# Router logits from widened embedding and hidden-turn matmuls, and the gating moved to earlier slots

## What is computed

```python
h = x_patch @ W.T + b                                   # embedding, D = 64
hid_t = tanh(layernorm(h) @ W_ih.T + b_ih + b_hh + hid_{t-1} @ W_hh.T)
h = h + hid_t                                           # called h2 in the kernel
x2 = layernorm(h)                                       # no scale, no shift
logits = x2 @ gate_w + gate_b                           # 16 experts
top2, idx = top_k(logits, 2); w = softmax(top2)
moe = sum_k w_k * (relu(x2 @ w1[idx_k] + b1[idx_k]) @ w2[idx_k] + b2[idx_k])
out = h + layernorm(x2 + moe) * gamma + beta
```

## Time and profile before

| | |
|---|---|
| three runs | 575.0 us median (574.65 to 578.51) |
| profiled execution | 573.36 us, of which its span is 571.6 us |
| mean granted TensorE clock | 0.987 |
| busy share of the span | PE 92%, DVE 75%, ACT 62%, POOL 27% |
| the chain that ended last | 86% PE, 5% DVE, 4% ACT |

### The profile page before, as it was taken

One profiled execution on the slowest core, in us unless ns is written; L12 is line 12 of the kernel. 1 busy time (PEld: TensorE's weight loads), 2 busy tenths in 40 slices (PEclk: granted clock), 3 DMA queues, 4 the chain that ended last, 5 costly groups with the idle time before them and its releaser, 6 DMA issues.

```text
span 571.6 us, 8948 instructions
## 1 busy us (share of the span) xinstructions
PE 526.4 (92%) x3138; PEld 358.3 (63%) x3138; DVE 428.4 (75%) x819; ACT 351.9 (62%) x596; POOL 155.2 (27%) x133
## 2 busy tenths in 40 slices
PE   2565999999999999999999999999999999989982
PEld 2355667667676767667676767666676766656541
DVE  1135787888888988788888888887878888786771
ACT  1244565666857585666757585666767585756552
POOL 4105021321314141331314141332214141221334
PEclk9999999999999999999999999999999999999995
DMA  3403865481909365482909375472909274563701
GB/s 79 100 1 79 194 139 120 103 183 49 234 24 198 85 148 133 100 179 57 227 22 203 80 155 118 116 171 62 224 20 210 75 160 104 122 145 91 168 1 42
DMA packets 30140, 67.45 MB, mean 118 GB/s; under 512 B 7056, under 2 KB 12432, under 8 KB 29968
## 3 DMA queue, kind: packets, MB, share of 16 engines
q1 hardware_dynamic: 30096, 66.89, 51.0%
HBM read 59.59 MB, written 7.28 MB: 117 GB/s over the span
## 4 chain that ended last, share of the span: by engine, by line
PE 86%; DVE 5%; ACT 4%; issue 2%; SPq 1%; POOL 1%; DMA 1%; POOLq 0%; DVEq 0%; ACTq 0%
PE pZ L711 32%; PE pO L724 31%; PE pA L735 4%; PE pA L660 4%; PE pB L635 4%; ACT hexp L426 2%; PE pA L653 2%; PE pB L686 2%; PE pA L675 2%; PE pA L645 1%; DVE acc L559 1%; PE pB L695 1%; SPq L293 1%; PE pB L675 1%; PE pA L654 1%
## 5 line engine op out<-in xcount | busy, mean ns | idle before, releaser
L426 ACT ACTIVATE hexp<-pZ,b1c 128x784 f32<-128x784 f32 x256 | 223.9, 909 | 105.2 <-PE pZ L711 105.0
L543 DVE SCALAR_TENSOR_TENSOR prod<-pO,b2c,spread 128x392 f32<-128x392 f32 x256 | 151.6, 623 | 85.2 <-PE pO L724 79.8
L724 PE MATMUL pO<-hexp,w2s 128*64 128x392 f32 x1024 | 198.5, 504 | 0.3 <-DVE prod L543 0.3
L711 PE MATMUL pZ<-xt,w1hi 128*128 128x392 f32 x512 | 191.3, 374 | 3.8 <-ACT hexp L426 2.7
L711 PE MATMUL pZ<-xt,w1lo 128*128 128x392 f32 x512 | 174.5, 341 | 0.0
L711 PEld LDWEIGHTS pZ<-xt,w1hi 128*128 128x128 f32 x512 | 96.7, 189 | 60.8 <-issue 28.1
L327 POOL TENSOR_TENSOR inv_std<-var,nhalf 112x7 f32<-112x7 f32 x48 | 75.1, 1572 | 216.0 <-DVE var L477 216.0
L559 DVE TENSOR_TENSOR acc<-acc,prod 128x784 f32<-128x784 f32 x112 | 121.0, 1080 | 0.1
L724 PEld LDWEIGHTS pO<-hexp,w2s 128*64 128x64 f32 x1024 | 70.0, 136 | 73.9 <-issue 62.2
L711 PEld LDWEIGHTS pZ<-xt,w1lo 128*128 128x128 f32 x512 | 97.1, 190 | 0.0
L334 POOL TENSOR_TENSOR h2b<-h2c,bet 112x448 f32<-112x448 f32 x16 | 17.4, 1087 | 145.2 <-DMA h2c<-h_dram 145.2
(11 more groups left out here) (74 smaller groups left out, 433.1 us busy)
## 6 DMA issues: line engine op xcount, KB each, us to landing
spread<-gates_dram SPq DMA_DIRECT2D x128, 392.0 KB, 8.6
h_dram<-h SPq DMA_DIRECT2D x16, 199.1 KB, 2.5
h2c<-h_dram SPq DMA_DIRECT2D x16, 199.1 KB, 8.2
xcur<-x_in SPq DMA_DIRECT2D x16, 196.0 KB, 8.1
out<-yo SPq DMA_DIRECT2D x16, 196.0 KB, 7.9
w1f<-w SPq DMA_DIRECT2D x2, 512.0 KB, 6.0
w2s<-w SPq DMA_DIRECT2D x1, 512.0 KB, 6.8
gates_dram<-gt SPq DMA_DIRECT2D x16, 28.0 KB, 2.0
```

Source lines behind the costliest of these rows:

```text
L426: nc.scalar.activation(hexp[u % RING][:, :].rearrange("p (b c) -> p b c", b=2), halves(pZ[u % 2]), ACT.Relu, bias=b1c[:, u:u + 1])\
L543: nc.vector.scalar_tensor_tensor(out=prod[q % RING][:, b * HALF:(b + 1) * HALF], in0=halves(pO)[:, b, :], scalar=b2c[:, q:q + 1], in1=spre ...
L711: last = nc.tensor.matmul(halves(pZ[e % 2])[:, b, :], w[:, e, :], xt[par][:, b * HALF:(b + 1) * HALF], start=(k == 0), stop=(k == 1))
L724: last = nc.tensor.matmul(halves(pO)[k * D:(k + 1) * D, b, :], w2s[:, e, :], hexp[e % RING][:, b * HALF:(b + 1) * HALF], start=True, stop= ...
```

## The change

The gate weights, centred, are appended to the matrices that embedding and hidden turn use, so that both write 16 more columns: the logits of h2 before it is divided by its standard deviation. The widened tiles (81 columns) don't fit one bank, so four tiles go to pA and three to pB, for both. DVE multiplies the 16 columns of h2 with the reciprocal deviation and adds the bias. The `logits` matmuls and the split of the gate weights go. `embed_in` moves from slot 7 to 9, `sum_turn` from 9 to 11, its copy on ACT from 10 to 12, `bias_logits` and `find_first` from 3 to 1, `find_second` from 5 to 3, the exponential from 6 to 4, `gate_weights` from 7 to 5, and `gates_turn` with the copy `gt` from 10 to 6. In bodies -2 and -1 the slots differ (`after(t, fill, steady)`).

```diff

+    W = D + 1 + E
-        tokw = sb("tokw", [K_IN + 1, D + 1])
+        tokw = sb("tokw", [K_IN + 1, W])
...
+        def wide_tile(i):
+            return wide_tiles(pA, PAIRS)[:, i, :] if i < PAIRS else wide_tiles(pB, TILES - PAIRS)[:, i - PAIRS, :]
+        wide_halves = ((slice(0, PAIRS), wide_tiles(pA, PAIRS)),
+                       (slice(PAIRS, TILES), wide_tiles(pB, TILES - PAIRS)))
...
                 if gate:
                     spread_gates(t + 1, 1 - par)
+                if mix and not known(t, 0):
+                    keep_h2(t + 2)
...
-                nc.scalar.activation(h1[par][:, :, :], tiles_and_mean(pB), ACT.Copy).then_inc(EMBED.sem, 1)
+                for some, fresh in wide_halves:
+                    nc.scalar.activation(h1[par][:, some, :], fresh, ACT.Copy).then_inc(EMBED.sem, 1)
+                    if gate and u == after(t, 3, 4):
+                        GATE.wait(act, t + 1, "diff")
+                        nc.scalar.activation(tv[:, 5, :], tv[:, 4, :], ACT.Exp).then_inc(GATE.sem, 1)
+                    if gate and u == after(t, 4, 6):
+                        GATE.wait(act, t + 1, "turned")
+                        ...
+                        nc.scalar.activation(gt[:, :], pB[0:2 * E, 0:FIRST], ACT.Copy).then_inc(GATE.sem, 1)
-                    if embed and u == after(t, 4, 7):
+                    if embed and u == after(t, 6, 9):
                         keep_h1(t + 3, 1 - par)
-                    if close and u == 10:
+                    if close and u == 12:
                         close_center(t - 1)
                         square(CLOSE, t - 1, "center", 2, cen[:, :, :])
...
             def bias_logits(s):
-                GATE.wait(dve, s, "logits")
-                nc.vector.tensor_tensor(lg[:, :, :], parts[:, 0, :, :], over_tiles(gbias[:, :], E), ALU.add)
+                MIX.wait(dve, s, "rstd")
+                nc.vector.tensor_tensor(lg[:, :, :], h2[:, :, D + 1:W], over_e(inv_std[:, 1, :]), ALU.mult)
-                nc.vector.tensor_tensor(lg[:, :, :], parts[:, 1, :, :], lg[:, :, :], ALU.add)
+                nc.vector.tensor_tensor(lg[:, :, :], lg[:, :, :], over_tiles(gbias[:, :], E), ALU.add)
-                    if gate and u == 3:
+                    if gate and u == 1:
                         bias_logits(g)
                         find_first(g)
+                    if gate and u == 3:
+                        find_second(g)
                     if gate and u == 5:
-                        find_second(g)
-                    if gate and u == 7:
                         gate_weights(g)
                     if mix and u == 7:
-                        nc.vector.tensor_tensor(h2[:, :, :], tiles_and_mean(pA), h1[par][:, :, :], ALU.add)
+                        for some, fresh in wide_halves:
+                            nc.vector.tensor_tensor(h2[:, some, :], fresh, h1[par][:, some, :], ALU.add)
...
             def embed_in(s):
-                    GATE.wait(pe, s - 2, "biased")
+                    MIX.wait(pe, s - 1, "h2")
             def hidden_turn(s):
                 MIX.wait(pe, s, "hid")
+                    GATE.wait(pe, s - 1, "gt")
-            def logits(s, par):
-                for i in range(TILES):
-                    last = nc.tensor.matmul(pB[0:P, i * 2 * E:(i + 1) * 2 * E], xt[par][:, i * P:(i + 1) * P],
-                                            gwhl[:, :], start=True, stop=True)
-                    if gate and u == 3:
-                        logits(t + 1, 1 - par)
-                    if gate and u == 10:
-                        gates_turn(t + 1, embed, close)
+                    if gate and u == after(t, 4, 6):
+                        gates_turn(t + 1)
-                    if embed and u == after(t, 4, 7):
+                    if embed and u == after(t, 6, 9):
                         embed_in(t + 3)
-                    if close and u == 9:
-                        sum_turn(t - 1, 1 - par, mix)
+                    if close and u == 11:
+                        sum_turn(t - 1, 1 - par, embed, mix)
```

More of the change, by code:

```diff
@@ L97, in vit_tower_kernel @@
         xcur = sb("xcur", [K_IN + 1, TOK])
-        h1 = [sb(f"h1_{i}", [P, TILES, D + 1]) for i in range(2)]
+        h1 = [sb(f"h1_{i}", [P, TILES, W]) for i in range(2)]
         xn1 = sb("xn1", [P, TILES, D])
         state = sb("state", [2 * D, 2, FIRST])
-        h2 = sb("h2", [P, TILES, D + 1])
+        h2 = sb("h2", [P, TILES, W])
         x2 = sb("x2", [P, TILES, D])
@@ L138, in wait @@
                 eng.wait_ge(self.sem, step * len(self.stages) + self.stages.index(stage) + 1)
-        EMBED = Chain("embed_stage", "h1 kept square var rstd norm turned xn1t_odd xn1t")
-        MIX = Chain("mix_stage", "pre hid_odd hid hid_turned h2 square var rstd x2 hi lo "
+        EMBED = Chain("embed_stage", "h1 kept_front kept square var rstd norm turned xn1t_odd xn1t")
+        MIX = Chain("mix_stage", "pre hid_odd hid hid_turned h2_front h2 square var rstd x2 hi lo "
                                  "turned_a turned_b xt_a xt_b")
-        GATE = Chain("gate_stage", "logits hi_part biased max1 hit1 ranked1 first1 best1 without "
+        GATE = Chain("gate_stage", "scaled biased max1 hit1 ranked1 first1 best1 without "
                                    "max2 hit2 ranked2 first2 best2 diff exp den p1 p2 g1 g2 gates turned gt")
@@ L214, in vit_tower_kernel @@
             cell_loads += [(cell[rows, k, :], w_ih), (cell[rows, 1 - k, :], w_hh),
-                           (rbias[rows, 0:1], b_ih.unsqueeze(1)), (rbias[rows, 1:2], b_hh.unsqueeze(1)),
-                           (gwf[rows, :], gate_w)]
+                           (rbias[rows, 0:1], b_ih.unsqueeze(1)), (rbias[rows, 1:2], b_hh.unsqueeze(1))]
             expert_loads += [(w1f[rows, :, :], w1)]
@@ L279, in body @@
                     fetch_h2(t - 1)
[L280 to L283, removed]
+                if known(t, 0):
+                    if mix:
+                        keep_h2(t + 2)
+                    if gate:
+                        load_x(t + 4)
                 if gate:
                     spread_gates(t + 1, 1 - par)
+                if mix and not known(t, 0):
+                    keep_h2(t + 2)
                 if close:
@@ L484, in bias_logits @@
             def bias_logits(s):
-                GATE.wait(dve, s, "logits")
-                parts = pB[0:P, 0:TILES * 2 * E].rearrange("p (i k e) -> p k i e", e=E, k=2)
-                nc.vector.tensor_tensor(lg[:, :, :], parts[:, 0, :, :], over_tiles(gbias[:, :], E), ALU.add)\
+                MIX.wait(dve, s, "rstd")
+                nc.vector.tensor_tensor(lg[:, :, :], h2[:, :, D + 1:W], over_e(inv_std[:, 1, :]), ALU.mult)\
                     .then_inc(GATE.sem, 1)
-                GATE.wait(dve, s, "hi_part")
-                nc.vector.tensor_tensor(lg[:, :, :], parts[:, 1, :, :], lg[:, :, :], ALU.add).then_inc(GATE.sem, 1)
+                GATE.wait(dve, s, "scaled")
+                nc.vector.tensor_tensor(lg[:, :, :], lg[:, :, :], over_tiles(gbias[:, :], E), ALU.add)\
+                    .then_inc(GATE.sem, 1)
             def find(s, k):
@@ L581, in body @@
                             dve.wait_ge(h2_stored, 16 * s)
-                        nc.vector.tensor_tensor(h2[:, :, :], tiles_and_mean(pA), h1[par][:, :, :], ALU.add)\
-                            .then_inc(MIX.sem, 1)
+                        for some, fresh in wide_halves:
+                            nc.vector.tensor_tensor(h2[:, some, :], fresh, h1[par][:, some, :], ALU.add)\
+                                .then_inc(MIX.sem, 1)
+                    if gate and u == 3:
+                        find_second(g)
                     if gate and u == 5:
-                        find_second(g)
-                    if gate and u == 7:
                         gate_weights(g)
@@ L621, in _ @@
             pe.wait_ge(consts, FOLD_SET)
-            nc.tensor.matmul(pA[0:K_IN + 1, 0:D + 1], tokt[:, :], fold[0:D, :], start=True, stop=True)\
-                .then_inc(tokw_made, 1)
+            for k in range(2):
+                last = nc.tensor.matmul(pA[k * D:(k + 1) * D, 0:E], fold[0:D, 0:D], gw[:, :], start=True, stop=True)
+            last.then_inc(weights_made, 1)
+            pe.wait_ge(weights_made, 2)
+            nc.tensor.matmul(pB[0:K_IN + 1, 0:W], tokt[:, :], fold[0:D, :], start=True, stop=True)\
+                .then_inc(weights_made, 1)
             pe.wait_ge(consts, ONES_SET)
-            pe.wait_ge(tokw_made, 2)
+            pe.wait_ge(weights_made, 4)
             def embed_in(s):
                 pe.wait_ge(xload, 16 * s + 16)
-                if not known(s, 2):
-                    GATE.wait(pe, s - 2, "biased")
-                elif not known(s, 1):
-                    EMBED.wait(pe, s - 1, "xn1t")
+                if not known(s, 1):
+                    MIX.wait(pe, s - 1, "h2")
                 for i in range(TILES):
```

(24 more changed lines are left out.)

44 lines of the change are left out of this document (17 added, 27 removed).

## The result

The changed kernel takes 660.5 us (four runs, 658.2 to 661.2) against 575.0 us beside it: 1.145 times the time of before, 95% interval 1.141 to 1.150. The forecast was 636 with a range to 658: the direction and the places were right, two prices too small.

A forecast was written before the change was run, and what follows sets the result against it. PE alone was taken to set the pace, 32.04 us per step. To the profiled 573.4 us came 48.9 (twelve full steps of +3.6, plus bodies 0, 13 and 14) and 14 for the clock: 636 us, range 604 to 658.

The forecast's parts named there:

- The gates' turn: Slot 6: PE is due at 10.1 us, DVE's gates are ready at 13.6, so PE stands 3.5 us per full step.
- 1.94 (318.93 to 320.87): Length in us taken for `find_second` in DVE's 12.6 us chain to the gates, from the rows of before.
- nobody waits: SP's queue: gate spread issued ahead of `keep_h2`; h2 is needed two bodies on, so no wait was expected.
- The clock: PE's granted clock falls in two in three of 14 stands, 1.5 us lost each, 1.0 per step: +14 us.
- Rival (b): PE's clock falls in every stall and takes long to come back: 656 us, chance 0.13.
- The closing norm: Slot 12: DVE stands 2 us for the closing square, PE about 1.1 before first layer 1; net +0.85 us per step.
- The logits and the wide columns: PE: removed logits matmuls gain 0.77 us in each of bodies 0 to 14; sixteen more columns cost 0.
- Fill and drain: Fill 0, between -3 and +3 us; body 0 +1.4, body 13 +2.7, body 14 +1.6.
- (a): The clock stays up because no stall is long enough to make it fall: 622 us, chance 0.25.
- (c): DVE's chain is shorter, gates come at 12.7 and the second stall goes: about 600 us, chance 0.10.
- (d): DVE's gates are ready in time and PE only loses the logits: 562 us, chance 0.05.
- (e): Wide columns cost their proportion, +0.69 us on 14 steps, 10 us on top of other cases; no chance of its own.

The follow-up runs named there:

- turn_10: Changed kernel with the gates' turn and its copy `gt` put back from slot 6 to slot 10: 587.9 us, 1.021 times the kernel before.
- beta_late: Changed kernel with POOL's two sums of h2 and beta moved behind its first power, from slot 4 to 11: 632.1 us, 1.097 times the kernel before.
- sum_first: Changed kernel with `sum_turn` put in slot 9 and `embed_in` in 11, gates' turn still in slot 6: 646.8 us, 1.125 times the kernel before.
- both_back: Changed kernel with the orders of `turn_10_exp_6` and `sum_first` together, wide tiles kept: 563.1 us, 0.979 times the kernel before.
- turn_10_exp_6: Changed kernel with gates' turn back in slot 10, exponential in slot 6, gate weights in slot 7: 577.0 us, 1.002 times the kernel before.

## Why the prediction missed its range

**The gates' turn.** Right in mechanism: DVE's chain without a pause, PE standing behind it, ended by DVE's gates, in each body. The stand was 4.10 us in the step shown and 4.0 on average over the full steps, for 3.5 forecast: 6 us in all. The term that failed is `find_second`, "1.94 (318.93 to 320.87)": it became 2.90. That row of before already held one slow instruction beside POOL's sum (0.72 us), and I took it as given, without asking where POOL's sums would go. They start when h2 has been fetched. The time from issue to landing, in the kernel before, the changed one and `turn_10`:

```profile
h2c<-h_dram SPq DMA_DIRECT2D x16, 199.1 KB, 8.2
...
h2c<-h_dram SPq DMA_DIRECT2D x16, 248.1 KB, 3.9
...
h2c<-h_dram SPq DMA_DIRECT2D x16, 248.1 KB, 6.9
```

The fetch is issued 6 us behind the last of the eight spreads in the kernel before, 18 us behind it in the changed one, and 8 in `turn_10`, where the spread is late again. So the shorter fetch goes with the earlier spread, and my sentence on SP, "nobody waits", overlooked that something also comes sooner. That POOL's place sets the length of the compares is shown by `beta_late`.

**The clock.** The step that failed is "I take two in three of 14, 1.0 per step: +14". The clock fell in all 15 stands, in three of them it stayed low twice as long, and filling the stand gave 24 us back, for 14 forecast. It is the term that was too small by most. A step with a long fall (body 7) beside one with a short fall (body 8):

```profile
317.86:357.24 39.38, 34.28 (x191) 22.34 (x190) 27.31 (x53) 22.09 (x40) 9.07 (x8) 0.91 0.46 107
357.24:395.28 38.04, 33.06 (x192) 21.22 (x190) 27.18 (x53) 22.11 (x40) 9.10 (x8) 0.96 0.48 110
```

The price of a short fall was right (1.5 taken, 1.66 and 1.6 measured), the count too low, and the long falls, 1.3 us more each, were not in it. The warning in the Trainium skill (TensorE: Matmul & The Clock Gate, "HAM oscillation — how this bites in real kernels") gave 21 by these prices and was the better guide: the clock fell in all 15 stands here. Rival (b), which had the clock fall every time but take long each time, named 656.

**The closing norm.** Right: DVE waited 1.89 us for the square, PE 0.94 for `hexp` 15, worth 0.86 per step by `sum_first` and 1.1 by `both_back` against `turn_10_exp_6`, for 0.85 forecast.

**The logits and the wide columns.** Right: `both_back` shows 0.65 gained per step, and 81 columns keep the pace of 65. Of the two rules in the Trainium skill (TensorE: Matmul & The Clock Gate), the one in "LDWEIGHTS (loading the stationary operand)" fits, with an estimate of 93 ns per record for 1.40/14 = 100 measured; the 6.7 ns more per record that "Back-to-back issue gap" would add are not seen in `hidden_turn` (1.40 for 1.42 us).

**Fill and drain.** Body 0 took 35.3 us for 30.6, where I had +1.4 and 1.0 for the clock. PE's first work of the body stands 2.6 us for x2 (1.1 before), the matmuls have their short duration only from 57.1 on (51.9 before), and at 67.3 the clock is down again. This term was too small by 2.3; the shares of these three are not taken apart.

In all, by the spans of the profiled executions: 12 full steps gave 75 us, forecast 43 and 12 for the clock; body 0 4.7; bodies 13 to 15 7.1, forecast 4.3 and 2; the fill 0.4, forecast 0. Rivals (a), (c), (d) and (e) are excluded by the same rows.

## What to carry to other kernels

When work is moved to earlier slots on one engine, add up that engine's program from the last point where it can still be waiting, and compare with the other's: an engine busy 80% of the time can have no slack at all where the slots are. A stand of PE of some 2 us or more may have to be priced twice, as time and as clock, unless something fills it: here the clock fell behind 2 of 7 stands of 2.0 us, 7 of 12 of 2.7, and all of 3.9 or more. When a transfer is moved, ask what now arrives sooner and beside whom it will run; two POOL instructions decided over 19 to 28 us here. The gain of a change may be real and hidden by its schedule: this one is worth 2% once its turns are put where nobody waits.

## What was unexpected of the hardware

- With stands of the same 2.7 us (`beta_late`, bodies 2 to 13), the granted clock fell in 7 of 12 and stayed in the others (36.7 and 35.2 us steps); with 3.9 us or more it fell in all. In body 0 of the changed kernel it fell behind a stand of only 2.0 us (idle to 66.24, fall at 67.3), where the same idle in body 0 of `sum_first` and in body 14 of the kernel before had none; and in body 13 a stand of 3.3 us had a fall in the changed kernel and none in `sum_first`. The length alone doesn't decide.
- Matmuls whose result is not used, in a stand, gave 24 us back (660.5 to 636.4).
- DVE's compares of 112 x 112 elements took 0.96 and 1.00 us beside POOL's sums and 0.28 without; its products, which read PSUM, kept their length (1.15 us at 320.87, with POOL's second sum running from 320.82).
